# A convolution mixer and eight experts on one core: pairs of gates, narrower matmul tiles, and a new order of steps

## What is computed

```python
x = x + conv_ref(ln_c(x), ...)             # mixer
t = tokens(x); t = t + ffn_ref(ln_t(t))    # experts
```

```python
for e in range(8):
    out += cw[:, e] * (gelu(xf @ W1[e] + b1[e]) @ W2[e] + b2[e])
```

## Time and profile before

| | |
|---|---|
| median of three runs | 169.97 us |
| profiled execution, its own time | 170.57 us |
| its span in the profile | 168.8 us |
| TensorE (PE) busy | 150.9 us, 89% |
| VectorE (DVE) busy | 111.4 us, 66% |
| ScalarE (ACT) busy | 96.4 us, 57% |
| GpSimd (POOL) busy | 81.7 us, 48% |
| granted TensorE clock | 0.99 on average, 1.00 until the last stretch |

### The profile page before, as it was taken

How to read it: one execution, slowest core, us unless ns; L and a number is a source line. 1 busy time by engine, 2 the same in 40 slices (tenths; PEclk the granted TensorE clock), 3 DMA queues, 4 the chain that set the end, 5 groups by cost and what they waited for, 6 DMA issues and landing times.

```text
span 168.8 us, 2942 instructions
## 1 busy us (share of the span) xinstructions
PE 150.9 (89%) x968; PEld 60.5 (36%) x968; DVE 111.4 (66%) x282; ACT 96.4 (57%) x186; POOL 81.7 (48%) x131
## 2 busy tenths in 40 slices
PE   6989998999999999599899997989998679799950
PEld 2443445553454454234344332432232222122210
DVE  1754947979799665699966689973638951353370
ACT  1653368537762679757276976475555448264610
POOL 7535330088033603465249863354548335486660
PEclk9999999999999999999999999999999999999996
DMA  3710600000000029910059700208940208940005
GB/s 102 187 16 8 186 0 0 6 2 2 0 4 0 0 39 216 219 35 2 0 124 217 167 0 4 62 10 196 214 91 0 64 8 184 214 99 0 0 4 124
DMA packets 8344, 11.84 MB, mean 70 GB/s; under 512 B 3842, under 2 KB 7306, under 8 KB 7306
## 3 DMA queue, kind: packets, MB, share of 16 engines
q1 hardware_dynamic: 7152, 11.05, 29.3%
q10 hardware_dynamic: 1178, 0.61, 1.5%
HBM read 10.48 MB, written 1.18 MB: 69 GB/s over the span
## 4 chain that ended last, share of the span: by engine, by line
PE 54%; DVE 21%; DMA 11%; issue 4%; ACT 3%; POOL 2%; SPq 1%; DVEq 0%; POOLq 0%; ACTq 0%
PE pm L1015 13%; DMA gates<-cwd 9%; PE pe L1015 5%; PE pe L1138 5%; PE pe L1125 4%; PE pm L1138 4%; PE pr L1142 3%; DVE tmp L910 3%; PE pm L1125 3%; DMA cwd<-cwS 2%; PE pm L1025 2%; DVE lg L672 2%; PE pr L1076 2%; DVE g L850 1%; PE pm L1054 1%
## 5 line engine op out<-in xcount | busy, mean ns | idle before, releaser
L455 POOL TENSOR_TENSOR acc<-acc,tmp 128x512 f32<-128x512 f32 x27 | 34.3, 1277 | 25.2 <-DVE tmp L910 24.9
L629 ACT ACTIVATE hid<-pe,b1T 128x512 f32<-128x512 f32 x48 | 30.2, 682 | 8.7 <-PE pe L1125 8.3
L1138 PE MATMUL pe<-hid,w 128*64 128x512 f32 x96 | 25.7, 611 | 3.4 <-DVE tmp L910 3.4
L1125 PE MATMUL pe<-fst,w 64*128 64x512 f32 x96 | 26.4, 625 | 0.5 <-ACT hid L629 0.4
L910 DVE SCALAR_TENSOR_TENSOR tmp<-pe,b2T,gates 128x512 f32<-128x512 f32 x24 | 17.9, 747 | 12.4 <-PE pe L1138 10.4
L1015 PE MATMUL pm<-pad,wT 64*128 64x512 f32 x108 | 25.1, 600 | 0.0
L629 ACT ACTIVATE hid<-pm,b1T 128x512 f32<-128x512 f32 x16 | 10.1, 684 | 11.9 <-PE pm L1125 8.3
L656 DVE SCALAR_TENSOR_TENSOR bcc<-bcp,cw_bc,bcc 128x256 f32<-128x256 f32 x32 | 15.6, 487 | 1.0
L391 POOL TENSOR_TENSOR r<-ve,halves 128x8 f32<-128x8 f32 x4 | 6.7, 1680 | 19.4 <-DVE ve L779 19.4
L1015 PEld LDWEIGHTS pm<-pad,wT 64*128 64x128 f32 x108 | 9.9, 185 | 11.3 <-issue 10.9
L476 ACT ACT_TABLE_LOAD x10 | 12.8, 1283 | 0.2
(11 more groups left out here) (225 smaller groups left out, 243.3 us busy)
## 6 DMA issues: line engine op xcount, KB each, us to landing
gates<-cwd SPq DMA_DIRECT2D x16, 512.0 KB, 8.3
xin<-in_x_dram SPq DMA_DIRECT2D x7, 128.0 KB, 3.0
out_dram<-acc SPq DMA_DIRECT2D x7, 128.0 KB, 2.6
w<-in_L_ffn_W_dram SPq DMA_DIRECT2D x2, 256.0 KB, 3.5
w<-in_L_ffn_W_dram ACTq DMA_DIRECT2D x1, 256.0 KB, 4.4
xin<-in_x_dram ACTq DMA_DIRECT2D x1, 128.0 KB, 2.8
cwd<-cwS SPq DMA_DIRECT2D x4, 32.0 KB
out_dram<-acc ACTq DMA_DIRECT2D x1, 128.0 KB, 2.4
```

What stands on the lines that cost most here:

```text
L455: pool.tensor_tensor(acc[p][:], (x2 if e == 0 else acc)[p][:], tmp[ln][e % 2][:], ALU.add).then_inc(summed[ln].sem, 1)
L629: act.activation(hid[ln][e % 2][:, q, :], expert_banks(g)[q][:], ACT.Gelu, bias=b1T[:, e:e + 1]).then_inc(hid_in[ln].sem, 1)
L1125: ins = pe.matmul(expert_banks(g)[q][:], w1[half, e, :], fst[p][half, :], start=True, stop=True)
L1138: ins = pe.matmul(expert_banks(g)[2][C * q:C * q + C, :], w2[:, e, :], hid[ln][e % 2][:, q, :], start=True, stop=True)
```

## The change

It has seven parts:
- `PLAN` has a new order of steps, and new tokens `sf20` to `sf23`.
- The gates are read back in four parts of two experts (`PARTS = 4`), so eight DMAs of 256 KB a group instead of four of 512 KB. `m0`, `m2`, `m4` and `m6` wait for one part each.
- The second layer `d` and the projection `pj` are four matmuls into 32 output columns each, instead of two into 64.
- The logits are read from their PSUM bank by the first routing operation; `ve2` copies 16 columns. So `pj` of the next group waits for that operation.
- The last three operations of the softplus (maximum with 0, add, multiply by exp(A)) leave POOL and become two of VectorE, step `sf2`.
- The last second layer (`d7` of group 3) goes by halves of its 512 columns into two banks; each half is weighed, added on VectorE and stored by itself.
- At the end SP issues the half-stores of group 3 ahead of the store of group 2.

```diff
-y13 a11 d21 cwc2 u41 m21 gs13 gw2 a21 ps3 h41 d31 stc3 stt3 u51 gst3 m31 pwg3 pj3 h51 d41 pc3 a31 u61 m41 rxg3
-rbg3 a41 h61 d51 x23 u71 m51 sq23 h71 s23 a51 d61 s2e3 t23 m61 u02 ve23 d71 h02 pw23 m71 u12 a61 rx23 rt03 d02
-h12 rb23 a71 m02 th3 u22 xn23 a02 st1 rt13 d12 h22 u03 rt23 u32 h03 m12 cwt3 cwc3 d03 h32 gw3 a12 d22 u13 m22
...
-m72 m73 a72 a73 st2 st3
...
+busy0 tr0 tT0 ini0 ve0 sq1 pw0 wa0 te0 tf0 wb0 rx0 dtv0 wae0 rb0 ex0 sm1 xn0 busy0 se1 sf00 bd0 ea0 cv00 bcp0
+nm0 sf10 wbe0 tr1 cv10 ve1 pw1 sf20 k00 cv20 rx1 k10 k20 rb1 xs00 busy0 dtv1 xs10 z0 bcs0 xn1 xt00 sz00 nT0 v00
+sz10 xt10 ne0 bt0 v10 bd1 btc0 kv0 bcp1 sq2 k01 cv01 kvc0 ex1 sq3 sf01 sm2 k11 sf11 y0 se2 cv11 y00 gs00 y10 tr2
+cv21 ve2 gs10 k21 pw2 ps0 xs01 sf21 dtv2 xs11 z1 stc0 rx2 stt0 xt01 gst0 sz01 rb2 c00 bcs1 pwg0 xn2 xt11 sz11
+v01 bd2 cf0 pj0 v11 bcp2 rxg0 k02 bt1 pc0 rbg0 cv02 x20 ex2 sf02 sq20 s20 k12 s2e0 btc1 t20 kv1 ve20 cv12 k22
+pw20 kvc1 bcs2 sf12 rt00 rx20 y1 cv22 y01 th0 rt10 rb20 xs02 xn20 z2 xs12 rt20 u00 sz02 sz12 xt02 y11 cwt0 gs01
+xt12 cwc0 bt2 sf22 gw0 gs11 pj1 v02 btc2 ps1 pc1 v12 stc1 kv2 stt1 kvc2 gst1 y2 h00 pwg1 sm3 y02 u10 se3 tr3 h10
+d00 ve3 rxg1 u20 pw3 m00 gs02 rbg1 h20 d10 x21 a00 rx3 u30 m10 sq21 rb3 dtv3 a10 s21 d20 xn3 s2e1 h30 t21 cv03
+ve21 y12 pw21 ex3 sf03 u40 cv13 rt01 sf13 h40 m20 th1 rx21 rt11 gs12 u50 rb21 a20 rt21 bd3 pj2 bcp3 xn21 d30 pc2
+k03 cwt1 h50 cv23 m30 cwc1 k13 gw1 a30 ps2 xs03 sf23 k23 xs13 z3 stc2 stt2 xt03 sz03 gst2 u60 sz13 v03 pwg2 bcs3
+xt13 bt3 v13 d40 btc3 rxg2 kv3 m40 rbg2 kvc3 a40 d50 x22 h60 y3 m50 sq22 u70 y03 a50 s22 h70 d60 s2e2 m60 gs03
+t22 u01 ve22 y13 d70 pw22 h01 m70 u11 a60 rx22 rt02 d01 h11 a70 rb22 m01 th2 u21 gs13 st0 rt12 a01 d11 h21 pj3
+xn22 rt22 u31 pc3 m11 cwt2 cwc2 h31 ps3 gw2 a11 d21 stc3 stt3 u41 gst3 m21 pwg3 h41 d31 a21 u51 rxg3 m31 rbg3
+h51 a31 d41 x23 u61 m41 sq23 h61 s23 a41 d51 s2e3 m51 t23 u71 ve23 d61 h71 pw23 m61 u02 a51 rx23 rt03 d71 h02
+a61 rb23 th3 u12 xn23 m71 u03 h12 rt13 a71 d02 h03 u22 st1 rt23 u13 h22 m02 cwt3 d03 cwc3 a02 h13 gw3 d12 u32
...
+d72 m63 a63 d73 m72 m73 a72 a73 st3 st2
...
+        def halves_of(step):
+
+            g = int(step[-1])
+            if step == LAST_DOWN:
+                return [(expert_banks(g)[2], slice(0, L)), (expert_banks(g)[0], slice(L, HT))]
+            return [(expert_banks(g)[2], slice(0, HT))]
+
+        def store_last(engine, q):
+
+            for b in range(2):
+                engine.wait_ge(summed[1].sem, summed[1].at(0, E + b))
+                engine.dma_start(out_v[NG - 1, q][:, b], acc[(NG - 1) % 2][C * q:C * q + C, L * b:L * b + L]
+                                 ).then_inc(d_out[(NG - 1) % 2].sem, 16)
...
-                    for part in range(2):
-                        es = slice(E // 2 * part, E // 2 * part + E // 2)
+                    for part in range(PARTS):
+                        es = slice(E // PARTS * part, E // PARTS * part + E // PARTS)
...
-                    pool.wait_ge(c.sem, c.at(g, 10))
-                    pool.tensor_tensor(dte[p][:], dte[p][:], dtm[p][:], ALU.add).then_inc(c.sem, 1)
...
+                elif step == "sf2":
+                    dve.wait_ge(dt_pool.sem, dt_pool.at(g, 9))
+                    dve.scalar_tensor_tensor(out=dtv[p][:], in0=dtv[p][:], scalar=0.0, in1=dte[p][:], op0=ALU.max,
+                                             op1=ALU.add).then_inc(dt_dve.sem, 1)
+                    if g == 0:
+                        dve.wait_ge(i_act, ACT_EXPA)
+                    if g > 1:
+                        dve.wait_ge(v_in.sem, v_in.at(g - 2, 2))
+                    dve.wait_ge(dt_dve.sem, dt_dve.at(g, 7))
+                    dve.tensor_tensor(dA[p][:], dtv[p][:], expA[:].unsqueeze(1).broadcast_to([P, NT, NH]),
+                                      ALU.mult).then_inc(dt_dve.sem, 1)
...
-                                      t2[p][:, 0, :, 2:2 + 2 * E].rearrange("p j (q e) -> p j q e", e=E),
+                                      pr[0][:, 2 * P:3 * P].rearrange("p (j r) -> p j r", r=BC)[:, :, 2:2 + 2 * E]
+                                      .rearrange("p j (q e) -> p j q e", e=E),
...
-                        pe.wait_ge(var_eps2.sem, var_eps2.at(g - 1, 1))
+                        pe.wait_ge(rt.sem, rt.at(g - 1, 1))
                     for q in range(2):
-                        ins = pe.matmul(pr[0][C * q:C * q + C, :], wo[:], g_[p][:, q, :], start=True, stop=True)
+                        for c in range(0, C, BC):
+                            ins = pe.matmul(pr[0][C * q + c:C * q + c + BC, :], wo[:, c:c + BC], g_[p][:, q, :], start=True,
+                                            stop=True)
...
-                    for q in range(2):
-                        ins = pe.matmul(expert_banks(g)[2][C * q:C * q + C, :], w2[:, e, :], hid[ln][e % 2][:, q, :],
-                                        start=True, stop=True)
-                    ins.then_inc(done[ln].sem, 1)
+                    for bank, half in halves_of(step + str(g)):
+                        for q in range(2):
+                            for c in range(0, C, BC):
+                                ins = pe.matmul(bank[C * q + c:C * q + c + BC, half], w2[:, e, c:c + BC],
+                                                hid[ln][e % 2][:, q, half], start=True, stop=True)
+                        ins.then_inc(done[ln].sem, 1)
```

More of the change, by code:

```diff
@@ L19 @@
 busy0 busy0 busy0 busy0 busy0 busy0 busy0 busy0 sq0 busy0 tb0 busy0 tw0 tap0 busy0 ta0 busy0 busy0 sm0 busy0 se0
[L20 to L28, removed]
@@ L183, in metaformer_block @@
         s2 = two("s2", [P, 2, P])
-        t2 = two("t2", [P, 2, TJ, 2 + 2 * E])
+        t2 = two("t2", [P, 2, TJ, 2])
         mq2 = two("mq2", [P, TJ, 2])
@@ L211, in metaformer_block @@
         cwd = [nc.dram_tensor(f"cwd{k}", [2 * E, HT], f32, kind="Internal").ap() for k in range(2)]
[L212 removed]
+        cwd_v = [t.rearrange("(q r e) t -> q r (e t)", q=2, r=PARTS) for t in cwd]
         cwd_t = [t.rearrange("m (j t) -> j m t", j=TJ) for t in cwd]
@@ L243, in metaformer_block @@
         d_cwd = count("d_cwd", 16)
-        d_gate = [[count(f"d_gate{k}{part}", 32) for part in range(2)] for k in range(2)]
+        d_gate = [[count(f"d_gate{k}{part}", 32) for part in range(PARTS)] for k in range(2)]
         d_out = [count(f"d_out{k}", 32) for k in range(2)]
@@ L353, in steps @@
                                      ).then_inc(d_out[p].sem, 16)
+                elif step == "st":
+                    store_last(sp, 0)
             walk(steps)
-            for k in range(2):
-                sp.wait_ge(d_out[k].sem, d_out[k].at(NG // 2 - 1, 32))
+            sp.wait_ge(d_out[0].sem, d_out[0].at(1, 32))
+            sp.wait_ge(d_out[1].sem, d_out[1].at(1, 64))
         @block.gpsimd
@@ L901, in steps @@
                     e, ln, n = WEIGH[step], lane(g), turn(g)
-                    if e % (E // 2) == 0:
-                        part = e // (E // 2)
+                    if e % (E // PARTS) == 0:
+                        part = e // (E // PARTS)
                         dve.wait_ge(d_gate[p][part].sem, d_gate[p][part].at(g // 2, 32))
@@ L908, in steps @@
                         dve.wait_ge(summed[ln].sem, summed[ln].at(n - 1, E + e - 1))
-                    dve.wait_ge(done[ln].sem, done[ln].at(n, e + 1))
-                    dve.scalar_tensor_tensor(out=tmp[ln][e % 2][:], in0=expert_banks(g)[2][:], scalar=b2T[:, e:e + 1],
-                                             in1=gates[p][:, e, :], op0=ALU.add, op1=ALU.mult).then_inc(gated[ln].sem, 1)
-                elif step + str(g) == LAST_ADD:
-                    dve.wait_ge(gated[1].sem, gated[1].at(0, E))
-                    dve.wait_ge(summed[1].sem, summed[1].at(0, E - 1))
-                    dve.tensor_tensor(acc[p][:], acc[p][:], tmp[1][(E - 1) % 2][:], ALU.add).then_inc(summed[1].sem, 1)
+                    for k, (bank, half) in enumerate(halves_of("d" + step[1:] + str(g))):
+                        dve.wait_ge(done[ln].sem, done[ln].at(n, e + 1 + k))
+                        dve.scalar_tensor_tensor(out=tmp[ln][e % 2][:, half], in0=bank[:, half], scalar=b2T[:, e:e + 1],
+                                                 in1=gates[p][:, e, half], op0=ALU.add, op1=ALU.mult
+                                                 ).then_inc(gated[ln].sem, 1)
+                        if step + str(g) == LAST_WEIGH:
+                            dve.wait_ge(gated[ln].sem, gated[ln].at(0, E + k))
+                            dve.wait_ge(summed[ln].sem, summed[ln].at(0, E - 1))
+                            dve.tensor_tensor(acc[p][:, half], acc[p][:, half], tmp[ln][e % 2][:, half],
+                                              ALU.add).then_inc(summed[ln].sem, 1)
             walk(steps)
```

49 lines of the change are left out of this document (18 added, 31 removed).

## The result

The changed kernel took 167.00 us (median of 4 runs, 166.91 to 167.59), the kernel before 169.81 us beside it (4 runs, 169.59 to 169.97). The ratio is 0.9843, 95% interval 0.9816 to 0.9870: 2.7 us faster by the ratio and 2.8 by the medians, where 4.5 had been forecast. The profiled execution after took 166.97 us, close to its median. That of before stood 0.8 us above the 169.81, so the two traces are 3.6 us apart, and 0.8 of this is between executions and not between kernels.

A forecast was written before the change was run, and what follows sets the result against it. TensorE, busy 150.9 of 168.8 us, was taken as the bound. Terms -2.7 - 1.2 - 4.3 + 0.5 + 0.5 + 2.4 + 0.3 = -4.5 us gave 165.5 by the median; own range 163.0 to 168.0, to 169.0 with A and B.

The forecast's parts named there:

- Gates, -2.7: Second-layer waits behind gate DMAs, groups 0 and 3: smaller transfers land earlier, removing 1.82 and 0.9 us.
- Tile sizes, -1.2: TensorE's steps: 107 instead of 115 tile-size changes at 0.15 us each, four 32-column tiles running together.
- Order, -0.9 net: TensorE's reordered steps: 4.3 us of waits removed, against new waits of 0.5, 0.5 and 2.4 us.
- six waits to be removed: TensorE waits at kv0, y3, ps3, u12, cwt3, d12, given filler by the new order: -4.3 us.
- those unseen, four of 0.6 us: New TensorE waits that couldn't be foreseen, sized by the average non-gate wait: +2.4 us, bounds 0 and 4.3.
- T2: Theory for the experiments that the new order only moves TensorE's waits; the same as A.
- Softplus and logits, 0: Softplus operations moved from POOL to VectorE cost nothing; PSUM logits only move the stall one line down, at best 0.23 us.
- Tail, +0.3: Last expert by halves: last add about 0.2 us earlier, but SP's last store starts at 166.0 instead of 165.7.
- A: Rival: the order only moves its waits, unseen ones eat the 4.3 us; +1.9, 167.4 us; chance 0.17.
- B: Rival: smaller gate transfers are slower, land no earlier, the 2.7 us stay; 168.2 us; chance 0.06.
- C: Rival: A and B together, 170.1 us, no change; chance 0.05.
- D: Rival, slower: VectorE stands before sf2 for POOL's late softplus chain; 171.3 us with the whole 5.8; chance 0.12.

The follow-up runs named there:

- four tiles alone: Kernel before, only second layer and projection changed to four matmuls of 32 columns: 169.28 us, ratio 0.9977 to the kernel before.
- pairs with tiles: Kernel before in its old order, with gates in four parts of two experts and four 32-column matmuls: 167.93 us, ratio 0.9896 to the kernel before.
- two tiles: Changed kernel with second layer and projection as two matmuls of 64 columns again: 167.82 us, ratio 0.9900 to the kernel before.
- pairs alone: Kernel before, only the gates changed, read back in four parts of two experts: 168.64 us, ratio 0.9945 to the kernel before.

## Why the prediction was right, and which terms were off

The sign and the range (163.0 to 169.0) held, and the mechanisms of the gates and the tiles did too; the size was 1.7 us too large. The range was wide, 6 us around a change of 4.5, and its lower end is not what its own terms give: 165.5 - 2.4 - 0.5 is 162.6.

**Gates, -2.7: the mechanism right, the size 1.9 in the new order and 0.9 in the old.** Both waits went, and a pair landed as early as forecast or earlier. The term that was mis-sized is "The waits to be removed are 1.82 and 0.9 us, so both go". It takes both prices from one execution, the profiled one, which took 0.8 us more than the median. The trace of the four tiles alone, with the same gates, has 0.26 us at the place of the 1.82. The sentence on what is late next held nearly: at the first place 0.18 us were left and 0.2 came back behind it. Stalls that are shorter in most executions would fit the 1.9 and 0.9 us of the runs; how long they are on average, no run shows.

**Tile sizes, -1.2: between 0.4 and 1.0 by the three comparisons** (four tiles alone, pairs to pairs with tiles, two tiles to after), none of which excludes the forecast. Four tiles of 32 columns run together, and the prices 1.00 and 0.86 held. That it is a little less than 8 x 0.15 is what the middles of the intervals say and no more.

**Order, -0.9 net: near in sum, and partly by luck.** From the pairs with tiles in the old order to the changed kernel the waits fall by 0.8 (9.8 to 9.0). The parts, by the timelines of before and after: of the six waits to be removed, `y3`, `u12`, `cwt3` and `d12` went whole and `kv0` fell from 0.46 to 0.15; only `ps3` still waits, 0.51 instead of 0.39 and now for `cwS`. That is 3.6 of the 4.3. The two new waits seen beforehand were 0.51 (`t20`, forecast 0.5) and 0.40 (`u10`, forecast 0.5). What failed is the term for those unseen, four of 0.6 us. Nine came, of 0.20 to 0.82 and together 4.5 us: `cwt2`, `d31`, `u03`, `d11`, `u11`, `u02`, a convolution step, `y2` and `t22`. Against them five waits of together 1.6 went that "I keep all the others" had kept. The net, 2.9, lies near the 2.4 because two misses cancel. All of TensorE's waits but the two for the gates add up in these timelines to 8.9 us before and 9.2 after, where the forecast had them fall by 0.9. So T2 is half right: beside the trace of before the order moved its waits, and its gain shows only against the variant with pairs and tiles.

**Softplus and logits, 0: right**, each undone by itself. The logits' stall moved down, as argued.

**Tail, +0.3: too small, 0.7.** The step that failed is "The last add ends about 0.2 us earlier relative to the last matmul step". It ended 0.6 later (3.56 us behind the start of that step instead of 2.98). I had halved the 1.01 of the earlier trace rows by size and had not asked which sums would run beside the first half. The prediction had the very stall, in its paragraph on the logits, and did not apply it here. The rest of the step, SP's queue putting group 2's stores last, was right.

With the sizes now known: 0.8 less from the gates, 0.4 less from the tiles (its middle 0.8), 0.4 more in the tail. That is 1.6 of the 4.5, and leaves 2.9, near the 2.8 between the medians. Of the signs named beforehand one did not come: TensorE's waits add up to 9.0 us and not to near 6.

**Rivals.** A (167.4) came nearest of them: the trace shows its picture of moved waits, with a little less lost. B fell: smaller transfers landed sooner. C fell with it. D fell: VectorE never stood before `sf2`.

## What to carry to other kernels

Read the price of a stall behind a DMA from more than one execution. Here the same wait was 1.82 us in one trace and 0.26 in another. Before calling a wait one that came back, look whether it stands behind the stall that was removed. Compare waits step by step and not by their line, and look whether a second producer is as late as the one that is named. In these runs, where a GpSimd sum ran beside VectorE, freeing one operation moved the stall to the next ones in the queue with two SBUF inputs. Go down the chain until none is left, and let a free bank hold one operand. Check the last microseconds for this separately: there the whole stall of 1.0 us was in the time.

## What the runs showed of the hardware that was not expected

The first two transfers of 256 KB of a group (runs of 4 KB) landed 3.4 to 4.5 us after their issues in groups 0 and 3 of four traces (after, pairs alone, pairs with tiles, two tiles). In the three traces with 512 KB (runs of 8 KB) the first landed after 4.5 to 5.3 us and the second after 6.4 to 8.3. One of these three has the new order (5.3 and 7.1 us, 4.5 and 6.4), so it is the size and not the order. The rates were 236 and 228 GB/s with pairs after the change and 227 and 222 before.

A VectorE operation of 0.22 to 0.23 us with one input in PSUM kept its time under a running GpSimd sum; with both in SBUF it took 1.03 and 1.12 us, and a 256-column addition 1.40 instead of 0.42. The Trainium skill (SBUF — State Buffer, Who interferes with whom) says that VectorE is blocked for the whole GpSimd instruction when both its inputs are in SBUF. The trace agrees: the operation of 1.03 us ends at 125.88, and the first of the two sums that began at 124.52 (2.69 us for both) ends half way, at about 125.87. What these runs add is the worth of the remedy in this kernel: 2.0 us for four groups' routing and 1.1 us for the additions at the end.
